# A decoder layer kernel: the first four batches' residual turned by DMA transposes, and the triangular mask of the last fourteen tiles written by ScalarE

## What is computed

```
x = layernorm(x + attention1(x))                 # 32 heads of 16, causal, with biases
x = layernorm(x + attention2(x, ctx, ctx, mask)) # 32 query heads, 8 key/value heads of 128, rotary positions
x = layernorm(x + ffn(x))                        # 4-bit weights: silu(x Wg) * (x Wu), then Wd, 1376 wide
```

## Time and profile before

| | before |
|---|---|
| time, median of 3 runs | 850.03 us (848.88 to 850.61) |
| time of the profiled execution | 849.92 us |
| its span, first to last instruction | 848.1 us |
| TensorE busy | 827.7 us, 98% |
| VectorE busy | 689.2 us, 81% |
| GpSimd busy | 632.8 us, 75% |
| ScalarE busy | 533.6 us, 63% |

### The profile page before, as it was taken

The page is one execution under the profiler, slowest core; times in us unless marked ns, Lnnn a source line. Parts: engine busy times, 40 slices in busy tenths (PEclk is TensorE's granted clock), DMA queues, the critical chain, the costliest instruction groups (busy, mean ns, idle before and its releaser), DMA issues.

```text
span 848.1 us, 17377 instructions
## 1 busy us (share of the span) xinstructions
PE 827.7 (98%) x6125; PEld 465.5 (55%) x6125; DVE 689.2 (81%) x1077; ACT 533.6 (63%) x1560; POOL 632.8 (75%) x563
## 2 busy tenths in 40 slices
PE   9899999999999999999999999999999999999997
PEld 4677777655555554555555555555555644434444
DVE  5688788998688778689788788798889755899897
ACT  5798888554765666576575676665666753777400
POOL 1199999897676686578777677578888633999896
PEclk9999999999999999999999999999999999999999
DMA  7675255103244422434425125213442223230011
GB/s 192 194 256 181 63 160 163 54 18 108 38 95 130 112 39 75 112 39 138 105 38 155 33 40 161 38 26 91 133 93 39 46 42 105 72 110 20 2 48 52
DMA packets 120038, 76.76 MB, mean 91 GB/s; under 512 B 72877, under 2 KB 104336, under 8 KB 119952
## 3 DMA queue, kind: packets, MB, share of 16 engines
q1 hardware_dynamic: 117504, 74.86, 33.5%
q10 hardware_dynamic: 2448, 0.79, 0.5%
HBM read 52.50 MB, written 6.36 MB: 69 GB/s over the span
## 4 chain that ended last, share of the span: by engine, by line
PE 62%; POOL 14%; DVE 7%; ACT 7%; issue 6%; DMA 3%; SPq 0%; POOLq 0%; ACTq 0%; DVEq 0%
PE bank L356 16%; PE bank L358 16%; PE bank L357 16%; POOL rot L647 2%; POOL left L680 2%; PE bank L1667 2%; POOL q2l L653 2%; POOL pn L664 2%; ACT prob L845 2%; POOL prob L657 2%; PE bank L1840 1%; PE bank L1841 1%; PE bank L1760 1%; PE bank L1759 1%; PE bank L1758 1%
## 5 line engine op out<-in xcount | busy, mean ns | idle before, releaser
L657 POOL TENSOR_TENSOR prob<-prob,rden 128x512 f32<-128x512 f32 x64 | 67.8, 1060 | 103.3 <-DVE rden L1318 103.0
L647 POOL TENSOR_TENSOR rot<-rcos,rsin 128x512 f32<-128x512 f32 x80 | 106.5, 1332 | 20.3 <-DVE rsin L1260 19.8
L356 PE MATMUL bank<-aTh,xqh 128*128 128x512 f16 x256 | 97.1, 379 | 1.4 <-DVE rsin L1260 0.9
L356 PE MATMUL bank<-xoh,o2h 128*128 128x512 f16 x256 | 97.1, 379 | 0.1
L357 PE MATMUL bank<-xol,o2h 128*128 128x512 f16 x256 | 97.2, 379 | 0.0
L358 PE MATMUL bank<-xoh,o2l 128*128 128x512 f16 x256 | 97.1, 379 | 0.0
L357 PE MATMUL bank<-aTl,xqh 128*128 128x512 f16 x256 | 97.1, 379 | 0.0
L358 PE MATMUL bank<-aTh,xql 128*128 128x512 f16 x256 | 97.1, 379 | 0.0
L1010 ACT ACTIVATE prob<-bank,ebias 128x128 f32<-128x128 f32 x256 | 90.4, 365 | 2.1
L1260 DVE SCALAR_TENSOR_TENSOR rsin<-bank,sinq 64x512 f32<-64x512 f32 x128 | 88.1, 688 | 1.7
L664 POOL TENSOR_TENSOR pn<-prob,pn 128x512 f16<-128x512 f32 x64 | 84.1, 1315 | 6.8 <-ACT pn L1022 6.6
(11 more groups left out here) (224 smaller groups left out, 2652.7 us busy)
## 6 DMA issues: line engine op xcount, KB each, us to landing
tst<-tables SPq DMA_DIRECT2D x11, 768.0 KB, 5.2
xqs<-in_xwq SPq DMA_DIRECT2D x8, 1024.0 KB, 6.6
xos<-in_xwo SPq DMA_DIRECT2D x8, 1024.0 KB, 5.6
qst<-in_fq SPq DMA_DIRECT2D x11, 384.0 KB, 3.4
kstk<-stack SPq DMA_DIRECT2D x48, 64.0 KB, 2.3
qstk<-stack SPq DMA_DIRECT2D x21, 128.0 KB, 2.6
xs<-in_ctxT SPq DMA_DIRECT2D x2, 1024.0 KB, 6.3
res<-in_x SPq DMA_DIRECT2D x1, 2048.0 KB, 8.4
```

The costliest lines, as they stand in the source:

```text
L356: pe.matmul(out_ap, ah, bh, start=first, stop=False)
L647: nc.gpsimd.tensor_tensor(rot[:, r % 2, :], rcos[:, r % 2, :], rsin[:, r % 2, :], ALU.add).then_inc(rope_rot, 1)
L657: nc.gpsimd.tensor_tensor(prob[:, v % 2, :].rearrange("p (h k) -> p h k", h=QH), prob[:, v % 2, :].rearrange("p (h k) -> p h k", h=QH), rd ...
```

## The change

Batches 0 to 3 leave the `t` fills. Their norm is applied by ScalarE, which then splits the high part off from `res` in SBUF into a small buffer `rows`; VectorE takes the low part from `res` and `rows`; SP turns each part with a DMA transpose straight into `aTh` and `aTl`. The `o` fills move one step forward, `v` from step 57 to 56, `k` from step 52 to 57. The mask of steps 50 to 63 is copied into the bank by ScalarE, two steps ahead, in place of the mask matmul.

```diff
+SEEDED = STEPS1 - 14
-    plan = [(STEPS1 - 12, "k", (0,)), (STEPS1 - 11, "o", (0,)), (STEPS1 - 10, "o", (1,)), (STEPS1 - 9, "t", (0, 0))]
-    plan += [(STEPS1 - 9, "o", (2,)), (STEPS1 - 8, "t", (0, 1)), (STEPS1 - 8, "o", (3,)), (STEPS1 - 7, "t", (0, 2))]
-    plan += [(STEPS1 - 7, "v", (0,)), (STEPS1 - 6, "t", (0, 3))]
+    plan = [(STEPS1 - 12 + b, "o", (b,)) for b in range(BH)]
+    plan += [(STEPS1 - 8, "v", (0,)), (STEPS1 - 7, "k", (0,))]
-SHIFTED = [(0, b) for b in range(BH, NB)]
+SHIFTED = [(0, b) for b in range(NB)]
...
+        rows = at(155.5, "rows", [P, 3, 2, D], F16)
...
+            def turn_rows(b):
+                if b == 0:
+                    sp.wait_ge(v1_psum, BLOCKS)
+                for i, (dst, done) in enumerate(((aTh, rows_hi), (aTl, rows_lo))):
+                    sp.wait_ge(done, b + 1)
+                    sp.dma_start_transpose(dst[:, :, b * S:(b + 1) * S], rows[:, b % 3, i, :]).then_inc(rows_in[b % 3], 16)
...
             load_kv(1)
+            for b in range(BH):
+                turn_rows(b)
             load_o(1)
...
+            def split_rows_hi(b):
+                act.wait_ge(ln_out, b + 1)
...
+                split_hi(rows[:, b % 3, 0, :], res[:, b, :], E_X).then_inc(rows_hi, 1)
+            def seed_triangle(u):
+                if u == SEEDED:
+                    act.wait_ge(consts_ready, 4)
+                act.wait_ge(exp_done, u - 1)
+                nc.scalar.copy(bank[2 + u % 2][:, :].rearrange("p (h k) -> p h k", h=4),
+                               tri[:, :].unsqueeze(1).to_broadcast([P, 4, S])).then_inc(seeded1, 1)
...
                 if 0 <= t < STEPS1:
                     exps1(t)
+                if SEEDED <= t + 2 < STEPS1:
+                    seed_triangle(t + 2)
                 if t >= STEPS1 - 2 and t < STEPS1:
                     seed_mask(t - STEPS1 + 2)
                 if 1 <= t <= STEPS1:
                     p1_hi(t - 1)
+                for layer, b in SHIFTED:
+                    if APPLY_SLOT[(layer, b)] == t:
+                        scaled_norm(layer, b)
+                        split_rows_hi(b)
...
+            def split_rows_lo(b):
+                dve.wait_ge(rows_hi, b + 1)
+                split_lo(rows[:, b % 3, 1, :], res[:, b, :], rows[:, b % 3, 0, :], E_X).then_inc(rows_lo, 1)
...
+                for b in range(BH):
+                    if APPLY_SLOT[(0, b)] == t:
+                        split_rows_lo(b)
                 weight_pieces(t - 1)
                 for f in fills_at(t):
                     if f not in turned_first(t):
                         consume(f)
...
-                pe_.matmul(dst, identb[:, :], tri[:, :].unsqueeze(1).to_broadcast([P, 4, S]), start=True, stop=False)
+                if u >= SEEDED:
+                    pe.wait_ge(seeded1, u - SEEDED + 1)
+                else:
+                    pe_.matmul(dst, identb[:, :], tri[:, :].unsqueeze(1).to_broadcast([P, 4, S]), start=True, stop=False)
...
                 if kind == "q":
-                    pe.wait_ge(fill_free, find_fill("t", 0, BH * ORDER[n][1] + BH - 1) + 1)
+                    if ORDER[n][1] == 0:
+                        for place in range(3):
+                            pe.wait_ge(rows_in[place], 32 * len(range(place, BH, 3)))
+                    else:
+                        pe.wait_ge(fill_free, find_fill("t", 0, NB - 1) + 1)
```

More of the change, by code:

```diff
@@ L231, in decoder_kernel @@
         power = sb("power", [P, 1], F32)
-        lnsh = sb("lnsh", [P, BH, 1], F32)
+        lnsh = sb("lnsh", [P, NB, 1], F32)
         scol16 = sb("scol16", [P, (NI - NSPLIT) * 2 * NK], F16)
@@ L321, in decoder_kernel @@
         k1_out, q1_out, q1_first, stack_in = sem("k1_out"), sem("q1_out"), sem("q1_first"), [sem("stack_in0"), sem("stack_in1")]
+        seeded1 = sem("seeded1")
         s_psum, nmax_done, ebias_done, exp_done = sem("s_psum"), sem("nmax_done"), sem("ebias_done"), sem("exp_done")
@@ L327, in decoder_kernel @@
             sem("ln_sum"), sem("ln_stat"), sem("ln_aggr"), sem("ln_ve"), sem("ln_rs"), sem("ln_out"))
+        rows_hi, rows_lo, rows_in = sem("rows_hi"), sem("rows_lo"), [sem(f"rows_in{i}") for i in range(3)]
         ln_shift, ln_mid, ln_right = sem("ln_shift"), sem("ln_mid"), sem("ln_right")
@@ L725, in inverse_sds @@
                 for (norm, b), slot in APPLY_SLOT.items():
-                    if norm == layer and slot == t + 1 and (norm, b) not in SHIFTED:
+                    if norm == layer and slot == t + 1 and (layer == 1 or slot < T0):
                         inverse_sd(layer * NB + b)
@@ L834, in v1_out @@
                                      ACT.Copy, scale=2.0 ** (E_V1 - E_X - E_W)).then_inc(v1_hi, 1)
+            def split_rows_hi(b):
+                act.wait_ge(ln_out, b + 1)
+                if b == 0:
+                    act.wait_ge(v1_psum, BLOCKS - 1)
+                if b >= 3:
+                    act.wait_ge(rows_in[b % 3], 32 * (b // 3))
+                split_hi(rows[:, b % 3, 0, :], res[:, b, :], E_X).then_inc(rows_hi, 1)
             def exps1(u):
@@ L962, in _, with scaled_norm @@
             w1_split_hi(0, 2)
+            def scaled_norm(layer, b):
+                e, r = layer * NB + b, res[:, b, :]
+                act.wait_ge(ln_shift, SHIFTED.index((layer, b)) + 1)
+                nc.scalar.activation(r, r, ACT.Identity, scale=lnrs[:, e % 3, :],
+                                     bias=lnsh[:, SHIFTED.index((layer, b)), :]).then_inc(ln_out, 1)
             for t in range(FIRST, T0):
@@ L994, in _ @@
                 rotations(fills_at(t - 1))
[L996 to L1000, removed]
             def exps(v):
@@ L1658, in scores1 @@
                     last = pe_.matmul(dst[:, 2 * i:2 * i + 2, :], qstk[0:3 * ROWS, j % 2, pair, t],
-                                      kstk[0:3 * ROWS, j % 2, :, pair, t], start=False, stop=(i == 1))
+                                      kstk[0:3 * ROWS, j % 2, :, pair, t], start=False, stop=(i == 1),
+                                      skip_group_check=(u >= SEEDED))
                 last.then_inc(s_psum, 1)
```

## The result

The changed kernel takes 858.78 us (median of 4, 857.70 to 859.40) against 850.32 us for the kernel before, run beside it: 1.0109 times [1.0094, 1.0123]. It is slower, by 8.5 us. The forecast was 859.9, range 854.0 to 865.5. The profiled execution took 858.56 us, its span is 856.4 us, mean granted clock 0.994.

What follows compares the result with a forecast made beforehand. TensorE, busy 98%, was the longest list by little; after the change the VectorE-ScalarE loop decides. 8.0 + 1.6 + 0.8 - 0.9 = +9.5, taken as +10.0 with hand-overs, on 849.92: 859.9 us, range 854 to 865.5.

Steps and rivals of the forecast that it cites:

- What leaves TensorE: Mask matmuls 3.0 us, transposes 1.9, waits at turned batches and first q 2.2: gain 7.1 us if nothing else waited.
- TensorE's list alone counts: Rival: PSUM's two-step lead covers all waits, so the kernel gets faster, 842.8 us; chance 0.05.
- The seeds: ScalarE's mask copies, steps 48 to 51: each moves what follows by 0.75 us; step 52 starts 1.2 us late.
- The loop: Steps 53 to 57: VectorE's and ScalarE's in-order lists wait for each other once per step, 6.85 us a turn.
- rival of a shorter loop: Rival: ScalarE reaches its norm earlier, turns take 5 us, the kernel is only 2.8 us slower, 852.7; chance 0.08.
- the way through GpSimd: GpSimd's inverse and weight piece per batch, 1.3 + 3.4 = 4.7 us, under 6.85, so said not to set the loop.
- Contention of the low part: VectorE's two-SBUF-input low part against GpSimd: 0 to 4.4 us, taken 0; rival with late landings 862 to 866, chance 0.10.
- The first q: First q fill, after step 59's scores: starts at 179.9 instead of 171.94, 8.0 us late.
- GpSimd late: From step 60, GpSimd 8 us later: 1.6 us before the last `turn1`, 0.8 for two fills in steps 63 and 64.
- The DMA transposes: Last low part's transpose lands at 180.1, together with the start of q: cost 0 to 4 us, taken as 0.
- The masks: Mask matmuls of steps 60 to 63 leaving TensorE give 0.9 us back.
- addition for hand-overs: Hand-overs between engines in steps 53 to 69 taken at twice 0.03 us: 0.5 us more, raising +9.5 to +10.0.

Runs made afterwards that it cites:

- seeds-alone: Kernel before, with the masks of steps 50 to 63 written by ScalarE and no batch turned differently: 850.60 us, ratio 1.0017.
- reordered kernel: Changed kernel with only the last four seeds, low part one step later behind the consumption, k ahead of v, output weight pieces later: 847.38 us, ratio 0.9972.
- two experiments: Changed kernel with all masks by matmul again, 857.98 us (1.0103); changed kernel with ScalarE's norm and high part ahead of `p1_hi`, 858.41 us (1.0107).
- TensorE kept busy: Changed kernel with 24 and 34 unused matmuls filling TensorE's waits in steps 56 and 58: 858.66 us, ratio 1.0104.
- pieces later alone: Changed kernel with GpSimd's output weight pieces of steps 60 and 61 moved to 65 and 66: 858.16 us, ratio 1.0108.

## Why the prediction was right

*What leaves TensorE* (7.1 us if nothing waits): right as a count. The seeds-alone and reordered runs show that it comes back only as far as no other list takes it. *TensorE's list alone counts*, 842.8, fell; even the reordered kernel stays 4.6 above it, of which the ten mask matmuls that it keeps are 2.2.

*The seeds*: step 52 was to start at 143.8 to 143.9, 6.7 to 6.8 us after the scores of step 49, and did so 6.81 after them (136.73 to 143.54). Alone they cost 1.4 us. A seed in the turn costs 0.52 with 1.17 behind the exponentials, 0.53 and 1.23 forecast, so it moves what follows by 0.68 and not 0.75.

*The loop*, the step that decides: forecast 6.85 (the ten terms as listed add up to 6.84), measured 6.80. Link by link, in the forecast's order, from the rows of the turn above: 0.95, 1.17, 0.52, 0.49, 0.83, 0.66, 0.64, 0.72, 0.72, 0.10. No link is off by more than 0.06. VectorE waits 1.91 to 3.36 us before the low parts ("about 3"), TensorE 0.95, 2.77 and 1.23 before o3, v and k ("1 to 3"). The rival of a shorter loop fell with it. What the step missed is that the loop is double: the way through GpSimd was dismissed with 4.7 of 6.85 us, counted to the end of the piece, without what follows when the low part has to wait for that end. That it changed no number here is luck: both ways happen to be equally long. It turned two experiments.

*Contention of the low part*, taken as 0 of 0 to 4.4: 0.69, 0.72, 0.73, 0.74 us, so 0 is right. But the reason, that GpSimd mostly waits when it runs, is wrong, and the 0 is luck: three of the four start in the last 0.2 us of the subtraction. With half a microsecond less in ScalarE's list each costs 0.5 to 0.7. (The far end of that rival, +16, is not worked out there; its two bounds of 4.4 and 4 add up to more.)

*The first q*: forecast 179.9, which is 42.8 after step 49's scores; measured 43.23. Two misses of opposite sign stand in it. The row maxima of step 57 were early, 39.54 for 39.99 (0.24 from the start of the loop, 0.2 from its turns). From there to q 3.69 us passed (176.27 to 179.96) where I had 2.8: 0.11 for a transpose of `onrm` that I left out, and most of the rest the clock, at 0.50 for the transposes of step 58 (0.90 from start to start for 0.47) and the scores (0.43 for 0.22).

*GpSimd late*, +2.4: from the first q to attention 2 it took 34.45 us, where the seeds alone, with the same masks gone, took 32.73 (173.16 to 205.89). That is 1.7 more, and the named cause is wrong in the changed kernel. TensorE does not wait there; what is paid is the q fill at half clock, eight matmuls of 0.43 and a part of the ninth, 1.72 us too much, which leaves the 32.73 of the seeds alone. With TensorE kept busy the same stretch lasts 34.95, 2.2 more than 32.73, and there it is mostly the wait for GpSimd's rotation that I forecast (TensorE's longest is 1.44 us). So the term was sized about right for the kernel with its clock up, 2.2 for 2.4, and the clock, for which the sum had no term, stood in its place. That the sum holds with it is luck.

*The DMA transposes*, cost 0: right. The last low part's was issued at 176.23 and landed some 2.5 us later, ahead of q. *The masks*, -0.9: in the 32.73 above (33.58 before).

In sum, from step 49 to attention 2: +8.4 at q, -0.9, +1.7, together the +9.3 measured, where the terms of the forecast made +9.5. The forecast total was 1.3 above the profiled execution: 0.2 by this, 0.5 by the addition for hand-overs, which were right as they stood, and the rest where the kernels are the same or outside the span. So the part that decides, the loop and the 8 us at q, was right in its mechanism; the 1.7 behind it was right in size alone.

## What to carry to other kernels

Where a step is moved between engines, write down each in-order list and look for a closed way through two of them; its length per turn, not the busy time of any engine, is then the time of a step, and it can be added up from start-to-start times of the trace to within 1%. Moving the waiting instruction behind what doesn't need it is worth more than removing instructions (3.7 us here for no work saved). Count a second way around too before you shorten the first, and move work only to where the receiving engine's list has a gap: the same seeds cost 1.4 us over fourteen steps and gain 0.9 in the last four.

## What the runs showed of the hardware

TensorE's granted clock falls to 0.50, the 1.2 GHz level, after waits of a few microseconds: in the changed kernel for 3.4 us behind the one of 2.77, and for 6.8 us from within the one of 3.99 on; in the reordered kernel, whose longest wait in this part is 1.29, it does not fall here. The same wait does not always end the same way: behind waits of 2.77 and 2.79 us in the run with the pieces later alone it stayed at 1.00. At 0.50 a 512-column matmul starts every 0.43 us for 0.217. The Trainium skill (TensorE: Matmul & The Clock Gate, Part 1: The HAM clock gate) says that the clock is halved when the engine has been little busy; the traces agree, and keeping it busy in the longest wait kept the clock at 1.00 from 176 on, though at no gain in the total.

A DMA transpose of 128x512 takes SP 1.19 to 1.30 us to issue, as much as one of 1024 columns, and lands in 2.4 to 4.2 us (median 2.5), where those took 3.0 to 7.4 (median 3.1).

VectorE's low part from two SBUF inputs takes 0.69 us where it meets no GpSimd instruction and 1.20 to 1.40 where it starts 0.3 to 0.5 us into GpSimd's subtraction of 1.15; its end is then some 0.55 us behind the subtraction's.
